# QKV weights in column blocks, made in their order of use while attention's first projections run

## The chip, the core and the metric

The kernel runs on one core of a Trainium2 chip. The core has five engines that work side by side, each through its own queue in order, and meet by semaphores: TensorE (PE in the profile; its weight loads are shown apart as PEld), VectorE (DVE), ScalarE (ACT), GpSimd (POOL) and SyncE (SP), which here issues the transfers. On-chip memory is SBUF (128 partitions); TensorE writes to PSUM. The metric is the device time of one execution in microseconds.

## The reference, cut to what matters

```python
# x: (8, 512, 1024) float32, H = 1024, 32 heads of 32
x = x + attention_a(layernorm(x), qkvw, qkvb, ow, ob)   # the stage of this change
x = x + ffn(layernorm(x), weight, bias, centroids, assignments)
x = x + attention_b(layernorm(x), bv_q, bv_k, bv_v)
x = x + ffn(layernorm(x), weight, bias, centroids, assignments)

def attention_a(x, qkvw, qkvb, ow, ob):
    q, k, v = split(x @ qkvw + qkvb)          # qkvw: (1024, 3072)
    probs = softmax(q @ k.T / sqrt(32))       # for each of 8 * 32 heads, 512 x 512
    return (probs @ v) @ ow + ob
```

## The kernel before

All products are made in float16 pairs. A float32 operand is scaled by a power of two and split into a high and a low half (hi = float16(s * w), lo = s * w - hi); a product of 128 x 512 by 1024 is then 24 matmuls (8 chunks of the contraction x 3 pairings of halves). The scale comes from the largest absolute value of the whole matrix: VectorE reduces each chunk (L255), GpSimd takes the maximum over partitions (partition_all_reduce, L231), VectorE makes the scale from it (scale_from_absmax, L71 to L75). The Q and K columns share one scale, the V columns have another.

**First phase** (L191 to L288). SyncE loads the weight in 8 row chunks for Q and K together (stg, 1 MB each, rows of 8 KB), then 8 for V (stgv, 512 KB each). VectorE reduces them; ScalarE writes the high halves (L285), VectorE the low ones (L245 for QK, L273 for V), GpSimd two of V's (L236, L238). They land in the arena, a buffer of 48 x 1024 float16 in each partition that all phases share: wqk in its parts 0 to 32, wv in 32 to 48. end_phase (L288) clears the semaphores and lets all engines meet.

**Second phase, attention** (from L291). SyncE asks for six tiles of x (128 x 1024 each, L501). For each: VectorE's bn_stats (L767) and bn_aggr, GpSimd's inv_deviation (L881, L883) and shift_x (L887), normalise_first on VectorE (L774), TensorE's transposes (turn_first, L622), ScalarE's hi_first (L689), VectorE's lo_first (L780, two operations a tile). Then TensorE runs the eight units of PRO: Q and K of head groups 0 and 1 (four units, L585), V of the first batch row, columns 0 to 512 (four units, L595). Each unit is 24 matmuls into the one bank proj_ps. ScalarE's leave (L681 for QK, L684 for V) copies it to stage, with the bias in bqk; GpSimd's split (L912, L914) makes the halves; SyncE stores and reloads those of Q and K for the heads. leave(u) of place i waits for the split of place i - 2; a unit waits until the bank is free (proj_free).

**Slots.** From there a hand-written schedule of one slot a head runs (SLOTS). Every slot has the score matmuls for the row maxima (max_scores, L536, banks ring_ps; VectorE L735), the scores (L546), the exponentials (ScalarE L666, L672; VectorE L753, GpSimd L859) and the weighted values (L563, L566); the projections of later groups (units_of) are laid between them, six matmuls at a time. Late in attention the output weight wo is loaded to the arena's parts 32 to 48, once the last V projection is done, and the feed-forward weight and small operands to parts 0 to 32, once the last Q and K projection is done.

GpSimd takes a partition_all_reduce also at L935 (late in attention) and L1396 and L1399 (in the stage behind it).

Of the kernel before, what the change touches and what calls it, by code (L numbers as in the profile page):

```python
# [127 lines left out]
def hybrid_layer(nc, x, qkvw, qkvb, ow, ob, bvq, bvk, bvv, fw, fb, cent, assign, out):  # L128
# [23 lines left out]
    with ExitStack() as top:  # L152
# [21 lines left out]
        def part16(a, z):  # L174
            return arena[:, a * H:z * H]
# [5 lines left out]
        wo = part16(32, 48).rearrange("p (a c n) -> p a c n", a=2, c=C)  # L181
        kq, signs, obias, cst, asg, asgf, ct0, fbx = (part32(2 * i, 2 * i + 2) for i in range(8))
        cst, asg, asgf, fbx = cst[0:NC], asg[0:NC].bitcast(I32), asgf[0:NC], fbx[0:33]
        fw_raw = part32(16, 32).rearrange("p (c n) -> p c n", c=C)


        with ExitStack() as p01:
            wqk = part16(0, 32).rearrange("p (a c n) -> p a c n", a=2, c=C)
            wv = part16(32, 48).rearrange("p (a c n) -> p a c n", a=2, c=C)
            bqk = sb(p01, "bqk", [P, 2 * H // P])  # L190
            exp_scale = sb(p01, "exp_scale", [P, 1])  # L191
            e_v = sb(p01, "e_v", [P, 1])
            s_v = sb(p01, "s_v", [P, 1])
# [4 lines left out]
            with ExitStack() as p0:  # L198
                stg = sb(p0, "stg", [P, C, 2 * H])
                stgv = sb(p0, "stgv", [P, C, H])  # L200
                mx = sb(p0, "mx", [P, 2, C + 1])
                bias = sb(p0, "bias", [P, 3 * H // P])
                m1 = sb(p0, "m1", [P, 2])
                m2 = sb(p0, "m2", [P, 2])
                es = sb(p0, "es", [P, 2])
                sc = sb(p0, "sc", [P, 2])
                qk_in, v_in, b_in = sem("qk_in"), sem("v_in"), sem("b_in")
                p0_max, p0_all, p0_sc, p0_hi, p0_id, p0_vs = (sem(n) for n in ("p0_max", "p0_all", "p0_sc", "p0_hi", "p0_id", "p0_vs"))
                V_LO_POOL = C // 4
                in_c = [sem(f"wc_in{c}") for c in range(C)]  # L210
                with nc.Block() as block:
                    @block.sync
                    def _(sp):
                        w_c = qkvw.rearrange("(c p) n -> c p n", p=P)
                        for c in range(C):
                            sp.dma_start(stg[:, c, :], w_c[c, :, 0:2 * H]).then_inc(in_c[c], 16)
                        for c in range(C):
                            sp.dma_start(stgv[:, c, :], w_c[c, :, 2 * H:3 * H]).then_inc(v_in, 16)

                    @block.gpsimd  # L220
                    def _(pool):
                        with nc.allow_non_contiguous_dma(reason="a small bias, one feature per partition"):
                            pool.dma_start(bias[:], qkvb.rearrange("(c p) -> p c", p=P)).then_inc(b_in, 16)
                        nc.gpsimd.memset(ident[:], 0.0).then_inc(p0_id, 1)
                        pool.wait_ge(p0_id, 1)
                        nc.gpsimd.affine_select(out=ident[:], in_=ident[:], compare_op=ALU.not_equal, fill=1.0,
                                                base=0, pattern=[[-1, P]], channel_multiplier=1).then_inc(p0_id, 1)

                        for i in range(2):
                            pool.wait_ge(p0_max, (C + 2) * (i + 1))  # L230
                            nc.gpsimd.partition_all_reduce(m2[:, i:i + 1], m1[:, i:i + 1], P, RMAX).then_inc(p0_all, 1)  # L231

                        pool.wait_ge(p0_sc, 6)
                        for c in range(V_LO_POOL):
                            pool.wait_ge(p0_hi, C + c + 1)
                            nc.gpsimd.tensor_scalar(stgv[:, c, :], stgv[:, c, :], sc[:, 1:2], None, ALU.mult).then_inc(p0_vs, 1)  # L236
                            pool.wait_ge(p0_vs, c + 1)
                            nc.gpsimd.tensor_tensor(wv[:, 1, c, :], stgv[:, c, :], wv[:, 0, c, :], ALU.subtract)  # L238

                    @block.vector  # L240
                    def _(dve):
                        def lo_qk(c):

                            dve.wait_ge(p0_hi, c + 1)
                            dve.scalar_tensor_tensor(out=wqk[:, 1, c, :], in0=stg[:, c, :], scalar=sc[:, 0:1],  # L245
                                                     in1=wqk[:, 0, c, :], op0=ALU.mult, op1=ALU.subtract)

                        for i, (w, b) in enumerate(((stg, bias[:, 0:2 * C]), (stgv, bias[:, 2 * C:3 * C]))):

                            for c in range(C):  # L250
                                if i == 0:
                                    dve.wait_ge(in_c[c], 16)
                                elif c == 0:
                                    dve.wait_ge(v_in, 16 * C)
                                dve.tensor_reduce(mx[:, i, c:c + 1], w[:, c, :], AX.X, ALU.max, apply_absolute_value=True).then_inc(p0_max, 1)  # L255
                            if i == 0:
                                dve.wait_ge(b_in, 16)
                            dve.tensor_reduce(mx[:, i, C:C + 1], b, AX.X, ALU.max, apply_absolute_value=True).then_inc(p0_max, 1)
                            dve.wait_ge(p0_max, (C + 2) * i + C + 1)
                            dve.tensor_reduce(m1[:, i:i + 1], mx[:, i, :], AX.X, ALU.max).then_inc(p0_max, 1)  # L260
                            dve.wait_ge(p0_all, i + 1)
                            scale_from_absmax(dve, m2[:, i:i + 1], es[:, i:i + 1], sc[:, i:i + 1], p0_sc, 3 * i)
                            if i == 0:

                                for c in range(C // 2):
                                    lo_qk(c)
                        dve.tensor_scalar(bqk[:], bias[:, 0:2 * C], sc[:, 0:1], None, ALU.mult)
                        for c in range(C // 2, C):
                            lo_qk(c)

                        for c in range(V_LO_POOL, C):
                            dve.wait_ge(p0_hi, C + c + 1)
                            dve.scalar_tensor_tensor(out=wv[:, 1, c, :], in0=stgv[:, c, :], scalar=sc[:, 1:2],  # L273
                                                     in1=wv[:, 0, c, :], op0=ALU.mult, op1=ALU.subtract)
                        dve.tensor_copy(e_v[:], es[:, 1:2])
                        dve.tensor_copy(s_v[:], sc[:, 1:2])
                        dve.scalar_tensor_tensor(out=exp_scale[:], in0=es[:, 0:1], scalar=float(HD) ** -0.5,
                                                 in1=es[:, 0:1], op0=ALU.mult, op1=ALU.mult)

                    @block.scalar  # L280
                    def _(act):
                        for i, (w, wd) in enumerate(((stg, wqk), (stgv, wv))):
                            act.wait_ge(p0_sc, 3 * (i + 1))
                            for c in range(C):
                                nc.scalar.activation(wd[:, 0, c, :], w[:, c, :], ACT.Copy, scale=sc[:, i:i + 1]).then_inc(p0_hi, 1)  # L285

            end_phase()


            with ExitStack() as p1:  # L290
                xt = sb(p1, "xt", [P, 2, H])  # L291
# [121 lines left out]
                def x_first(t):  # L413
                    two = (e32[:], ehi[:].rearrange("p a t s -> p a (t s)").bitcast(F32).rearrange("p a (h s) -> p a h s", h=2),
                           elo[:].rearrange("p a t s -> p a (t s)").bitcast(F32).rearrange("p a (h s) -> p a h s", h=2))[t // 2]
                    return two[:, t % 2].rearrange("p h s -> p (h s)")
# [7 lines left out]
                with nc.Block() as block:  # L424

                    @block.sync
                    def _(sp):
                        def load_x(n):
                            if n >= FIRST + 2:
                                sp.wait_ge(proj_full, place["T", n - 2, 1] + 1)  # L430
                            sp.dma_start(xt[:, n % 2], x_t[n // T, n % T]).then_inc(xt_in, 16)
# [31 lines left out]
                        def out_weight(s):  # L463
# [17 lines left out]
                            if 0 <= c < C:  # L481
                                sp.wait_ge(proj_full, place["V", B - 1, T - 1, 1] + 1)
                                sp.wait_ge(wo_out, 16 * C)
                                sp.dma_start(wo[:, :, c], wo_d[c]).then_inc(wo_in, 16)
# [15 lines left out]
                        for t in range(FIRST):  # L500
                            sp.dma_start(x_first(t), x_t[t // T, t % T]).then_inc(x0_in[t], 16)  # L501
# [1580 lines left out]
```

## Time and profile before

| | |
|---|---|
| median of 3 runs | 3384.23 us (3383.88 to 3388.84) |
| the profiled execution | 3387.1 us, span 3385.3 us |
| granted TensorE clock over the span | 0.99 |
| TensorE busy | 3205.6 us, 95% |
| VectorE, ScalarE, GpSimd busy | 65%, 52%, 57% |
| first phase | 0 to 73.7 us |
| last stage, chain that ended last | TensorE |

The profile lists each engine's instructions with start and duration in us from the span's start. A group names line, engine, operation, written tile and read tiles. "Idle before" is the time in which the engine stood still ahead of an instruction, with what released it. The granted clock (PEclk) is in shares of TensorE's full speed.

### The profile page before, as it was taken

How to read it: one execution, taken by the hardware profiler on the slowest of the kernel's cores; microseconds unless marked ns; L12 is line 12 of the kernel's file. 1: busy time of each engine (PE TensorE's matmuls, PEld its weight loads, DVE VectorE, ACT ScalarE, POOL GpSimd, SP SyncE). 2: the span in 40 equal slices, each digit the busy share in tenths (PEclk: the TensorE clock that was granted, in tenths of full speed). 3: DMA queues.
4: the chain of work that ended last, by engine and by line, in shares of the span. 5: the costliest groups of instructions: out<-in, count | busy, mean ns of one | idle time of the engine just before them, and what ended most of it. 6: DMA issues, size and time to landing. Idle time of an engine off the chain costs nothing. (4 is left out here: it accounts for less than half of the span.)

```text
span 3385.3 us, 62616 instructions
## 1 busy us (share of the span) xinstructions
PE 3205.6 (95%) x24256; PEld 1711.9 (51%) x24256; DVE 2189.8 (65%) x3858; ACT 1745.6 (52%) x2125; POOL 1927.5 (57%) x2065
## 2 busy tenths in 40 slices
PE   0899999999999999999999899998999999999999
PEld 0455555555555555555444455554555555554443
DVE  8377777777777777777788587774455555542311
ACT  3277777777777777777677422221345555552000
POOL 2277777777777777777676422221565555540422
PEclk9999999999999999999999899999999999999999
DMA  4122222222222222222334644443223222223533
GB/s 186 41 60 70 67 70 68 78 64 70 72 64 70 64 73 64 76 70 69 108 111 140 192 166 158 156 157 112 75 88 104 102 100 100 88 76 144 204 137 137
DMA packets 277524, 342.95 MB, mean 101 GB/s; under 512 B 92236, under 2 KB 206924, under 8 KB 276206
## 3 DMA queue, kind: packets, MB, share of 16 engines
q1 hardware_dynamic: 272558, 322.16, 30.0%
q10 hardware_dynamic: 4608, 16.78, 1.3%
q8 instruction: 194, 3.18, 0.4%
q14 instruction: 100, 0.82, 0.1%
q0 software_dynamic: 64, 0.01, 0.0%
HBM read 199.91 MB, written 138.42 MB: 100 GB/s over the span
## 5 line engine op out<-in xcount | busy, mean ns | idle before, releaser
L735 DVE TENSOR_REDUCE nmax<-ring_ps 128x1 f32<-128x512 f32 x1024 | 676.2, 685 | 418.2 <-PE ring_ps L536 415.6
L859 POOL TENSOR_TENSOR elo<-e,ehi 128x1024 f16<-128x1024 f32 x256 | 669.6, 2616 | 355.7 <-ACT ehi L672 355.7
L666 ACT ACTIVATE e<-st_ps,exp_scale 128x1024 f32<-128x1024 f32 x512 | 570.7, 1115 | 373.2 <-PE st_ps L546 308.2
L585 PE MATMUL proj_ps<-xnT,arena 128*128 128x512 f16 x3072 | 750.5, 381 | 3.3 <-DVE xnT L780 2.5
L672 ACT ACTIVATE ehi<-st_ps,exp_scale 128x1024 f16<-128x1024 f32 x512 | 568.6, 1110 | 0.0
L1596 PE MATMUL f_ps<-wT,fxT 128*128 128x512 f16 x1920 | 435.6, 381 | 2.9 <-DMA fxT<-xT_scratch 2.9
L585 PEld LDWEIGHTS proj_ps<-xnT,arena 128*128 128x128 f16 x3072 | 272.3, 97 | 286.9 <-ACT stage L684 11.7
L536 PE MATMUL ring_ps<-ks,qs 96*128 96x512 f16 x1024 | 397.2, 388 | 17.0 <-DVE nmax L735 17.0
L546 PE MATMUL st_ps<-qs,ks 98*128 98x512 f16 x1024 | 392.6, 383 | 12.0 <-ACT ehi L672 11.3
L563 PEld LDWEIGHTS ctx_ps<-v_sb,ehi 128*128 128x128 f16 x4096 | 312.5, 97 | 155.1 <-DVE sums L762 39.3
L563 PE MATMUL ctx_ps<-v_sb,ehi 128*128 128x65 f16 x4096 | 372.0, 192 | 14.0 <-DVE sums L762 12.7
L595 PE MATMUL proj_ps<-arena,xnT 128*128 128x512 f16 x1536 | 370.8, 378 | 2.9 <-ACT stage L684 2.1
L566 PE MATMUL ctx_ps<-v_sb,elo 128*128 128x33 f16 x4096 | 355.8, 179 | 0.0
L1086 PE MATMUL o_ps<-arena,cT 128*128 128x512 f16 x1536 | 344.0, 381 | 3.2 <-DVE cT L1315 3.2
L753 DVE TENSOR_TENSOR elo<-e,ehi 128x1024 f16<-128x1024 f32 x256 | 333.3, 1302 | 1.1 <-ACT ehi L672 1.1
L566 PEld LDWEIGHTS ctx_ps<-v_sb,elo 128*128 128x128 f16 x4096 | 274.7, 97 | 116.1 <-issue 3.1
L1596 PEld LDWEIGHTS f_ps<-wT,fxT 128*128 128x128 f16 x1920 | 187.4, 98 | 208.8 <-issue 6.0
L1086 PEld LDWEIGHTS o_ps<-arena,cT 128*128 128x128 f16 x1536 | 149.8, 98 | 172.9 <-DVE cT L1315 4.0
L2019 POOL TENSOR_TENSOR arena<-arena,fm 128x512 f32<-128x512 f32 x64 | 83.6, 1306 | 229.3 <-DVE fm L1872 229.3
L595 PEld LDWEIGHTS proj_ps<-arena,xnT 128*128 128x128 f16 x1536 | 135.4, 97 | 144.0 <-ACT stage L684 3.5
L1386 POOL TENSOR_SCALAR rstd<-mv 128x1 f32<-128x1 f32 x32 | 7.1, 223 | 301.1 <-DVE mv L1264 286.6
L536 PEld LDWEIGHTS ring_ps<-ks,qs 96*128 96x128 f16 x1024 | 115.8, 113 | 97.4 <-DVE nmax L735 34.5
(240 smaller groups left out, 4616.3 us busy)
## 6 DMA issues: line engine op xcount, KB each, us to landing
qk_scratch<-qk_hl SPq DMA_DIRECT2D x128, 256.0 KB, 2.3
fxT<-xT_scratch SPq DMA_DIRECT2D x64, 512.0 KB, 3.5
qs<-qk_scratch SPq DMA_DIRECT2D x192, 128.0 KB, 2.6
ks<-qk_scratch SPq DMA_DIRECT2D x192, 128.0 KB, 2.9
arena<-x_scratch SPq DMA_DIRECT2D x48, 512.0 KB, 4.3
ctx_scratch<-ctx SPq DMA_DIRECT2D x64, 256.0 KB, 3.0
xb<-in_L_attn_a_x_dram SPq DMA_DIRECT2D x32, 512.0 KB, 4.4
x_scratch<-xb SPq DMA_DIRECT2D x32, 512.0 KB, 2.6
```

What stands on the lines that cost most here:

```text
L536: pe.matmul(ring_ps[:, ring_max(h, c) % 2, :], qs_v[0:3 * HD, h % RING, c, :], ks[0:3 * HD, h % RING, :], start=True, stop=True).then_inc( ...
L546: mm = pe.matmul(st_ps[:, c // 2, c % 2, :], ks[0:3 * HD + 2, h % RING, P * c:P * c + P], qs[0:3 * HD + 2, h % RING, :], start=True, stop= ...
L563: pe.matmul(ctx_v[:, t, :], ehi[:, h % 2, c, P * t:P * t + P], v_sb[:, c, hh, :], start=(c == 0 and t == 0), stop=False, skip_group_check= ...
L566: mm = pe.matmul(ctx_v[:, t, 0:HD + 1], elo[:, h % 2, c, P * t:P * t + P], v_sb[:, c, hh, 0:HD + 1], start=False, stop=(c == T - 1), skip_ ...
L585: mm = pe.matmul(proj_ps[:], wqk[:, wp, c, H * qk + P * g:H * qk + P * g + P], xnT[:, b % 2, xp, c, :], start=(n == 0), stop=(n == 23))
L595: mm = pe.matmul(proj_ps[:], xnT[:, b % 2, xp, c, P * t:P * t + P], wv[:, wp, c, S * half:S * half + S], start=(n == 0), stop=(n == 23))
L666: nc.scalar.activation(e32[:, half], st_ps[:, half], ACT.Exp, scale=exp_scale[:, 0:1]).then_inc(e32_done, 1)
L672: nc.scalar.activation(ehi[:, h % 2, 2 * half:2 * half + 2, :], st_ps[:, half], ACT.Exp, scale=exp_scale[:, 0:1]).then_inc(ehi_done, 1)
L735: dve.tensor_reduce(nmax[:, h % 2, c:c + 1], ring_ps[:, ring_max(h, c) % 2, :], AX.X, ALU.max, negate=True).then_inc(ring_free, 1)
L859: nc.gpsimd.tensor_tensor(elo[:, h % 2, 2:4, :], e32[:, 1], ehi[:, h % 2, 2:4, :], ALU.subtract).then_inc(elo_pool, 1)
L1086: mm = pe.matmul(o_ps[:, half, :], cT[:, n % 2, xp, c, :], wo[:, wp, c, 512 * half:512 * half + 512], start=(i == 0), stop=(i == 23))
L1596: pe.matmul(f_ps[:, half, :], fxT[:, t % 2, xp, c, :], wT[:, wp, c, cols], start=(n == 0), stop=False)
```

## The change

The first phase goes; its work is done inside attention's block. The weight is cut into six column blocks, BLOCKS = QK 0, V 0, QK 1, V 1, QK 2, QK 3. A QK block holds 256 columns of Q and 256 of K (two head groups), a V block 512 columns. Block j has its halves in the arena's parts 8j to 8j + 8, and its raw float32 data, loaded ahead, in the place of block j + 1 (the last one in e32 and ehi). It is worked in two halves of 128 x 2048: weight_hi(j) on ScalarE, weight_lo(j) on VectorE; the high half of block j + 1 overwrites raw data of block j and waits for its low half.

SyncE asks for x tiles 0 to 3 first, then for the eight QK pieces, then the four V pieces (1 MB each; 1 KB runs for QK, 2 KB for V), then for x tiles 4 and 5. The layer norm's normalise_first goes from VectorE to ScalarE. The V scale is made once block QK 0 is finished. Units wait for their own block only (qkv_lo). Two banks take turns in PRO (proj_ps and ring_ps 1), so that a unit waits for the leave of the one before the last; the slots wait until all eight are left. The memset of ks goes to GpSimd. The output weight (wo_part) now lies in the places of the V blocks and the feed-forward weight in parts 32 to 48, under the same waits as before.

```diff
-        wo = part16(32, 48).rearrange("p (a c n) -> p a c n", a=2, c=C)
-        fw_raw = part32(16, 32).rearrange("p (c n) -> p c n", c=C)
+        def wo_part(c):
+            return part16(8 + 16 * (c // 4), 16 + 16 * (c // 4)).rearrange("p (a c n) -> p a c n", a=2, c=4)[:, :, c % 4]
+        fw_raw = part32(32, 48).rearrange("p (c n) -> p c n", c=C)
...
+            BLOCKS = (("QK", 0), ("V", 0), ("QK", 1), ("V", 1), ("QK", 2), ("QK", 3))
+            def half_of(j, i, a):
+                return part16(8 * j + 4 * i + 2 * a, 8 * j + 4 * i + 2 * a + 2)
...
-            end_phase()
...
+                def bank(u):
+                    return ring_ps[:, 1] if place[u] < len(PRO) and place[u] % 2 else proj_ps[:]
...
-                        for t in range(FIRST):
+                        for t in range(T):
                             sp.dma_start(x_first(t), x_t[t // T, t % T]).then_inc(x0_in[t], 16)
+                        for n, (j, i) in enumerate(LOADS):
+                            piece = raw_of(j, i).rearrange("p (c n) -> p c n", c=C if BLOCKS[j][0] == "QK" else C // 2)
+                            sp.dma_start(piece, raw_from(j, i)).then_inc(qkv_in[n], 16)
+                        for t in range(T, FIRST):
+                            sp.wait_ge(x0_turned, 2 * (t - T) + 2)
+                            sp.dma_start(x_first(t), x_t[t // T, t % T]).then_inc(x0_in[t], 16)
...
                         for i, u in enumerate(PRO):
                             unit(u, 0, 24)
-                            if i < 2:
-                                turn_first(T + i)
-                        pe.wait_ge(const_done, 4)
+                            if i in (3, 4):
+                                turn_first(T + i - 3)
+                        pe.wait_ge(const_done, 3)
+                        pe.wait_ge(ks_ones, 1)
                         pe.wait_ge(x0_lo, 2 * FIRST)
+                        pe.wait_ge(qkv_lo, 2 * NB)
+                        pe.wait_ge(proj_free, len(PRO))
...
+                        def weight_hi(j):
+                            v = BLOCKS[j][0] == "V"
+                            act.wait_ge(p0_sc, 6 if v else 3)
+                            for i in range(2):
+                                wait(act, qkv_lo, 2 * (j - 1) + i + 1)
+                                nc.scalar.activation(half_of(j, i, 0), raw_of(j, i), ACT.Copy, scale=sc[:, v:v + 1]).then_inc(qkv_hi, 1)
...
+                        weight_hi(0)
+                        act.wait_ge(bqk_done, 1)
+                        leave(PRO[0])
+                        weight_hi(1)
+                        leave(PRO[1])
+                        normalise_first(4)
+                        normalise_first(5)
+                        weight_hi(2)
+                        leave(PRO[2])
+                        leave(PRO[3])
+                        hi_first(4)
+                        weight_hi(3)
+                        leave(PRO[4])
+                        hi_first(5)
+                        weight_hi(4)
+                        leave(PRO[5])
+                        weight_hi(5)
+                        leave(PRO[6])
+                        leave(PRO[7])
...
+                        for t in range(T):
+                            stats_first(t)
+                        for n in range(C):
+                            weight_max(n)
+                            if n < T:
+                                lo_first(n)
+                        weight_scale(0)
...
+                        weight_lo(0)
+                        for n in range(C, C + 4):
+                            weight_max(n)
+                        weight_scale(1)
+                        weight_lo(1)
+                        stats_first(4)
+                        stats_first(5)
+                        weight_lo(2)
+                        lo_first(4)
+                        weight_lo(3)
+                        lo_first(5)
+                        weight_lo(4)
+                        weight_lo(5)
...
+                        def weight_all(kind):
+                            pool.wait_ge(p0_max, C + 8 if kind else C + 2)
+                            nc.gpsimd.partition_all_reduce(m2[:, kind:kind + 1], m1[:, kind:kind + 1], P, RMAX).then_inc(p0_all, 1)
...
+                        nc.gpsimd.memset(ks[3 * HD:3 * HD + 2], ONES_ROW).then_inc(ks_ones, 1)
+                        pool.wait_ge(ks_ones, 1)
+                        weight_all(0)
+                        split(PRO[0])
+                        weight_all(1)
+                        split(PRO[1])
+                        for t in range(T, FIRST):
+                            inv_deviation(t)
+                            shift_x(t)
+                        for u in PRO[2:]:
                             split(u)
```

## Rows read from the trace of the kernel before

**Rows 1.** The page: span, busy tenths in 40 slices, one of its groups.

```profile
span 3385.3 us, 62616 instructions
...
PE   0899999999999999999999899998999999999999
...
L585 PEld LDWEIGHTS proj_ps<-xnT,arena 128*128 128x128 f16 x3072 | 272.3, 97 | 286.9 <-ACT stage L684 11.7
```

**Rows 2.** Windows: stretch and length, busy us by engine, clock, DMA share, GB/s.

```profile
200.00:1600.00 1400.00, 1387.12 (x12134) 737.31 (x12131) 1061.99 (x1928) 1014.08 (x1054) 1084.32 (x1103) 1.00 0.24 69
```

**Rows 3.** Timeline, 0 to 75 us: start, us, engine, line, operation [idle before].

```profile
13.18 2.29 DVE L255 TENSOR_REDUCE mx<-stg 128x1 f32<-128x2048 f32 x1 [0.64 <-DMA stg<-_L_attn_a_attn_qkvw_dram]
...
25.64 2.29 DVE L255 TENSOR_REDUCE mx<-stg 128x1 f32<-128x2048 f32 x1 [0.22 <-DMA stg<-_L_attn_a_attn_qkvw_dram]
...
29.31 15.25 ACT L285 ACTIVATE arena<-stg,sc 128x2048 f16<-128x2048 f32 x8 [27.23 <-DVE sc L75]
31.42 9.14 DVE L245 SCALAR_TENSOR_TENSOR arena<-stg,sc,arena 128x2048 f16<-128x2048 f32 x4 [2.14 <-ACT arena L285]
...
49.94 0.35 POOL L231 PARTITION_ALL_REDUCE m<-m  x1 [21.23 <-DVE m L260]
...
50.88 8.43 ACT L285 ACTIVATE arena<-stgv,sc 128x1024 f16<-128x1024 f32 x8 [6.32 <-DVE sc L75]
...
73.69 0.80 SPq L501 DMA_DIRECT2D e<-in_L_attn_a_x_dram  x2
```

**Rows 4.** Timeline, 75 to 147 us.

```profile
78.27 1.29 DVE L767 BATCH_NORM_STATS2 st<-e 128x6 f32<-128x512 f32 x2
...
81.00 0.27 POOL L887 TENSOR_SCALAR shift<-mv,rstd 128x1 f32<-128x1 f32 x1
...
84.34 1.28 DVE L780 TENSOR_TENSOR xnT<-st_ps,xnT 128x512 f16<-128x512 f32 x2
...
95.61 7.85 PE L585 MATMUL proj_ps<-xnT,arena 128*128 128x512 f16 x24 [2.54 <-DVE xnT L780]
...
104.24 5.35 PE L585 MATMUL proj_ps<-xnT,arena 128*128 128x512 f16 x24
104.25 0.61 POOL L912 CAST qk_hl<-stage 128x512 f16<-128x512 f32 x1 [8.82 <-ACT stage L681]
...
104.95 1.16 POOL L914 TENSOR_TENSOR qk_hl<-stage,qk_hl 128x512 f16<-128x512 f32 x1
...
109.43 1.04 PE L622 MATMUL st_ps<-ident,elo 128*128 128x128 f32 x8
...
145.97 0.60 PE L536 MATMUL ring_ps<-ks,qs 96*128 96x512 f16 x2
```

**Rows 5.** Line 694, the norm of later x tiles on ScalarE: ns min/median/max.

```profile
L694 ACT ACTIVATE xt<-xt,shift,rstd x26: 1235/1238/1254, 191.9 to 1554.0; 128x1024 f32<-128x1024 f32 x26
```

**Rows 6.** Timeline of GpSimd around its all-reduces.

```profile
57.50 5.31 POOL L236 TENSOR_SCALAR stgv<-stgv,sc 128x1024 f32<-128x1024 f32 x1 [7.22 <-ACT arena L285]
...
1675.31 0.38 POOL L935 PARTITION_ALL_REDUCE m2o<-m1o  x1 [5.88 <-issue]
...
1683.21 1.14 POOL L914 TENSOR_TENSOR qk_hl<-stage,qk_hl 128x512 f16<-128x512 f32 x1 [6.98 <-issue]
...
2050.06 0.38 POOL L1399 PARTITION_ALL_REDUCE m<-m  x1 [8.14 <-issue]
```

**Rows 7.** Windows of TensorE alone: stretch, length, busy, clock, DMA share, GB/s.

```profile
152.00:154.00 2.00, 2.00 (x5) 0.50 0.08 1
...
1684.00:1688.00 4.00, 0.00 (x0) 0.56 0.39 111
```

**Rows 8.** Windows of all engines in the old load and behind attention.

```profile
13.20:33.20 20.00, 0.00 (x0) 0.00 (x0) 16.17 (x12) 3.89 (x3) 0.38 (x1) 1.00 1.01 417
...
1960.00:2060.00 100.00, 100.00 (x692) 56.14 (x691) 78.29 (x137) 21.33 (x48) 24.05 (x25) 1.00 0.49 164
```

**Rows 9.** Line 273, VectorE beside GpSimd: ns min/median/max.

```profile
L273 DVE SCALAR_TENSOR_TENSOR arena<-stgv,sc,arena x6: 1273/2095/3137, 60.1 to 69.6; 128x1024 f16<-128x1024 f32 x6
```

More of the change, by code:

```diff
@@ L190, in hybrid_layer, with wv @@
+            def wv(half, a, c):
+                return half_of(BLOCKS.index(("V", half)), c // 4, a)[:, S * (c % 4):S * (c % 4) + S]
             bqk = sb(p01, "bqk", [P, 2 * H // P])
             exp_scale = sb(p01, "exp_scale", [P, 1])
-            e_v = sb(p01, "e_v", [P, 1])
-            s_v = sb(p01, "s_v", [P, 1])
             e_o = sb(p01, "e_o", [P, 1])
             bv_hl = sb(p01, "bv_hl", [P, 2, C], F16)
[L198 to L285, printed above, removed]
@@ L573, in unit @@
                             if a == 0:
-                                wait(pe, proj_free, place[u])
+                                wait(pe, proj_free, place[u] - 1 if place[u] < len(PRO) else place[u])
                             if u[0] == "QK":
@@ L588, in unit @@
                                 b, t, half = u[1:]
+                                if a == 0 and b == 0:
+                                    pe.wait_ge(qkv_lo, 2 * BLOCKS.index(("V", half)) + 2)
                                 if a == 0 and half == 0 and T * b + t < FIRST:
@@ L594, in unit @@
                                     c, (xp, wp) = n // 3, ((0, 0), (0, 1), (1, 0))[n % 3]
-                                    mm = pe.matmul(proj_ps[:], xnT[:, b % 2, xp, c, P * t:P * t + P],
-                                                   wv[:, wp, c, S * half:S * half + S], start=(n == 0), stop=(n == 23))
+                                    mm = pe.matmul(bank(u), xnT[:, b % 2, xp, c, P * t:P * t + P],
+                                                   wv(half, wp, c), start=(n == 0), stop=(n == 23))
                             if z == 24:
@@ L633, in turn @@
                             mm.then_inc(proj_full, 1)
+                        pe.wait_ge(p0_id, 2)
                         for t in range(T):
@@ new lines, in weight_scale @@
+                        def weight_scale(kind):
+                            k, done = (C, C + 2) if kind == 0 else (4, C + 8)
+                            if kind == 0:
+                                dve.wait_ge(b_in, 16)
+                            dve.tensor_reduce(mx[:, kind, k:k + 1], bias[:, 2 * C * kind:2 * C * kind + (C if kind else 2 * C)], AX.X, ALU.max,
+                                              apply_absolute_value=True).then_inc(p0_max, 1)
+                            dve.wait_ge(p0_max, done - 1)
+                            dve.tensor_reduce(m1[:, kind:kind + 1], mx[:, kind, 0:k + 1], AX.X, ALU.max).then_inc(p0_max, 1)
+                            dve.wait_ge(p0_all, kind + 1)
+                            scale_from_absmax(dve, m2[:, kind:kind + 1], es[:, kind:kind + 1], sc[:, kind:kind + 1], p0_sc, 3 * kind)
@@ new lines, in weight_lo @@
+                        def weight_lo(j):
+                            v = int(BLOCKS[j][0] == "V")
+                            for i in range(2):
+                                dve.wait_ge(qkv_hi, 2 * j + i + 1)
+                                dve.scalar_tensor_tensor(out=half_of(j, i, 1), in0=raw_of(j, i), scalar=sc[:, v:v + 1],
+                                                         in1=half_of(j, i, 0), op0=ALU.mult, op1=ALU.subtract).then_inc(qkv_lo, 1)
+                        for t in range(T):
+                            stats_first(t)
@@ L914, in split @@
                             nc.gpsimd.tensor_tensor(lo, src, hi, ALU.subtract).then_inc(split_done, 1)
+                        def weight_all(kind):
+                            pool.wait_ge(p0_max, C + 8 if kind else C + 2)
+                            nc.gpsimd.partition_all_reduce(m2[:, kind:kind + 1], m1[:, kind:kind + 1], P, RMAX).then_inc(p0_all, 1)
+                        with nc.allow_non_contiguous_dma(reason="a small bias, one feature per partition"):
+                            pool.dma_start(bias[:], qkvb.rearrange("(c p) -> p c", p=P)).then_inc(b_in, 16)
+                        nc.gpsimd.memset(ident[:], 0.0).then_inc(p0_id, 1)
+                        pool.wait_ge(p0_id, 1)
+                        nc.gpsimd.affine_select(out=ident[:], in_=ident[:], compare_op=ALU.not_equal, fill=1.0,
+                                                base=0, pattern=[[-1, P]], channel_multiplier=1).then_inc(p0_id, 1)
                         pool.wait_ge(const_done, 1)
-                        for t in range(FIRST):
+                        for t in range(T):
                             inv_deviation(t)
                             shift_x(t)
-                        for u in PRO:
+                        pool.wait_ge(shift_done, T)
+                        nc.gpsimd.memset(ks[3 * HD:3 * HD + 2], ONES_ROW).then_inc(ks_ones, 1)
[8 more added lines that the diff above has]
+                        for u in PRO[2:]:
                             split(u)
```

95 lines of the change are left out of this document (61 added, 34 removed).

## The prediction

> **What bounds the kernel now.** The page first: TensorE is busy for eight or nine tenths of every slice but the first [rows 1]; in the long middle of attention it works for 1387 of 1400 us [rows 2]. So a time saved elsewhere counts only where TensorE has nothing to do, and that is the first slice. The timeline of the first 150 us shows it. Until 73.7 us the first phase brings the whole QKV weight, finds its largest values and splits it; only then is x asked for [rows 3], and the first projection runs at 95.61. Eight projections in a row follow, and the first score matmul, from which on TensorE sets the pace, starts at 145.97 [rows 4]. I forecast that mark for the changed kernel; what follows it is the same work in the same order, bound by TensorE, so I let the end move by as much.
>
> **Load and largest value.** x (2 MB) now goes first, then the QK pieces of 1 MB. Before, the third megabyte was in use at 13.18 [rows 3], so the first QK piece is there at 13.2 (the arrivals before it are an estimate: 4.4 to 10.2 for x, from the 4.6 us that x0 took from its request at 73.69 to its statistics at 78.27 [rows 3, 4] and 1.25 to 1.5 us for each half megabyte). VectorE now also does lo_first (two operations, 1.28 us [rows 4]) behind each of the first four reductions. The reductions take 2.29 us [rows 3], so the eighth starts at 13.2 + 7 x 2.29 + 4 x 1.28 = 34.3. The layer norm of x fits ahead of that (3.0 us from statistics to shift [rows 4]), except that the third and fourth turn wait for lo_first(0) and (1); nobody waits for them before 44. What it costs if the load is slower: the last QK piece must be there at 34.3, which leaves 3.0 us for each megabyte. Packets shrink from 8 KB to 1 KB. In the old load the queues moved 417 GB/s at full share (2.5 us a megabyte); the stage behind attention, with many small packets, 164 GB/s at a share of 0.49, so 335 (3.1 us) [rows 8]; attention 69 at 0.24, so 288 (3.6 us) [rows 2]. I take at most 3.0, nearest the middle row, so no cost; the bounds are 0 and 5.3 us. From the start of the last reduction to ScalarE's first split before: 25.64 to 29.31, 3.67 us [rows 3]. So ScalarE starts on block 0 at 38.0, VectorE 2.11 us later [rows 3], and two lo operations of 2.3 us end at 44.7. The constants moved to GpSimd (ks memset) lie in its idle time between 13 and 34.
>
> **First projection at 44.7 instead of 95.6.** It started on a slow clock before: 24 matmuls in 7.85 us against 5.35 for the next [rows 4]. TensorE now idles for over 20 us ahead of it, so I take 7.85 again (bounds 5.35 and 10.4, all 24 at twice the 0.216 us of the fast ones, 104.24 to 109.43 [rows 4]): end 52.6. ScalarE's leave lies between that and GpSimd's split (103.46 to 104.25 before), which takes 1.86 us (to 106.11 [rows 4]): 55.2.
>
> **The wait that the change adds.** GpSimd's queue is now weight_all(0), split(PRO[0]), weight_all(1), split(PRO[1]), the norm of x tiles 4 and 5. The trace shows that GpSimd stands still whenever it goes from ordinary work to PARTITION_ALL_REDUCE or back. Toward it: 5.9 us (ahead of 1675.31) with the DMA queues quiet, 8.1 at 2050.06 with them busy. Back: 7.2 at 57.50 although ScalarE's piece, the named releaser, was ready at 52.0 (50.88 + 1.1 [rows 3]), and 7.0 at 1683.21 [rows 6]. The old kernel ran its two all-reduces back to back and paid one such stop, in the shadow of VectorE. The new one puts a split between them. The V reductions (4 x 2.29 behind 44.7) and the small ones are done at 54.3, but the all-reduce waits for the split until 55.2 and then for the stop of 5.9: 61.1 (bounds 0, were the stop hidden, and 8.1; I take 5.9 because the weight load is over by then). Behind it are queued: ScalarE's weight_hi(1), thus leave(PRO[1]), thus projection 3; VectorE's lo(1), then the statistics of x tiles 4 and 5. The stops around all-reduce 0 are hidden: toward it between 20 and 34, back between 38 and 53.3.
>
> By the Trainium skill's page "GPSIMD Engine Reference", section 2.1 (Instruction dispatch), the first call of a freshly loaded GpSimd routine pays about 6 us with nothing to see in the profile. Read strictly, the second all-reduce is no first call and would pay nothing (rival 1); but the third and the fifth of this trace, at 1675 and 2050, pay in full [rows 6], so I side with the rows.
>
> **From there to the mark.** ScalarE starts block 1 at 61.1 + 0.94 = 62.0 (49.94 to 50.88 before [rows 3]). VectorE's second lo ends at 62.0 + 2.1 + 4.6 = 68.7. Statistics of tile 4 from 68.7 and of tile 5 from 70.2, shift 3.0 us on (78.27 to 81.27 [rows 4]): 73.2. GpSimd's stop back ends at 61.5 + 7.0 = 68.5 and its split at 70.4, just in time. The norm now runs on ScalarE at 1.24 us [rows 5], and sits ahead of weight_hi(2) and leave(PRO[2]) in its queue: norm 5 ends at 74.4, two splits of 1.95 at 78.3, leave(PRO[2]) at 79.0. Projection 2 ended long before (about 63), yet projection 4 must wait for that bank: it starts at 79.0. Projection 3 and the turn of tile 4 (1.04 us) end by 74.5, so TensorE has 4.5 idle us. Before, the short score matmuls from 145.97 on, each waiting for VectorE, were followed by a granted clock of 0.50 (152 to 154), and an idle stretch at 1684 to 1688 by 0.56, partly at the lower level [rows 7]; that level is 1.2 GHz, full is 2.4. I take the slow 7.85 for projection 4 (bounds 5.35 and 10.4): 86.9. Turn 5: 87.9. Projections 5 to 7 use alternate banks, so the leave between two projections (0.8 us) is gone: 3 x 5.2 (104.24 to 109.43 [rows 4]) = 15.6, end 103.5. Leave of the last, 0.2 + 0.6, which now must end before the first score matmul because it shares a bank with it: mark at 104.5. VectorE's lo chain and ScalarE's weight_hi(3) to (5) fit in beside: the last lo is due about 100.7. Their slack is some 3 us; GpSimd's splits can eat of it, since lo operations that took 1.27 us alone took up to 3.14 beside GpSimd [rows 9].
>
> **Sum:** 145.97 - 104.5 = 41.5 us less. Nothing else is priced: the barrier of 1 us is inside it, and the new places of the output and feed-forward weights in the arena keep their waits. The profiled execution took 3387.1 us, 2.9 above the median of 3384.2; I forecast the median: 3384.2 - 41.5 = 3342.7.
>
> **Rivals.**
> 1. The stop does not land on the path (no stop, or hidden behind another chain): 5.9 less, and the clock may stay up at projection 4, 2.5 less: 3334 to 3340. For it: at 49.94 an all-reduce paid nothing, but right behind another one [rows 3]. Against: each all-reduce that follows ordinary work pays [rows 6]. 10%.
> 2. The 1 KB load is the bound: at 3.1 to 3.6 us a megabyte the scale is late by 1 to 5.3 us: 3344 to 3348; with the 8.1 stop 3350. For it: the two rows with small packets. Against: those rows mix reads and writes, and the pieces here only read. 20%. By the Trainium skill's page "DMA: Bandwidth & Descriptors", Specifications, packets from 512 B up go at line rate, which would rule this rival out; no row here shows 1 KB reads alone.
> 3. The other side, slower: the projections read their weights from blocks with another stride, those of Q and K are 3072 matmuls, nearly all inside attention [rows 1]. LDWEIGHTS takes 97 ns and hides under a matmul of 216. If each grew by over 15.7 ns ((41.5 + 6.8) / 3072), the kernel would be over 0.2% slower; at 20 ns 3384.2 - 41.5 + 61.4 = 3404. Against: width, type and contiguity of what one LDWEIGHTS reads stay. 2%.
> 4. The change does not do what it says: the chains of block 1 to 5 on VectorE and ScalarE hold the projections so long that the mark hardly moves, or attention hands the gain back to something tied to the clock: 3384. It would take 40 us of delay beyond the worked chain, which counts all of the 24 large operations. 2%.
> The forecast, with its own bounds of the clock and the stop (3339 to 3346), has the remaining 66%.
>
> **Range.** From 3336 (into rival 1, and the old load shows a lull from 7 to 9 us that may fall elsewhere, 2 us) to 3350 (rival 2): 80%. A measurement of this kernel can tell about 0.2%, 6.8 us, from no change. Faster by more than that: 66 + 10 + 20% = 96%; same 2%; slower 2%.
>
> **What would show it.** First projection at 45 (load and VectorE chain); an all-reduce at 61, a gap of about 6 us in front of it and of 7 behind it; ScalarE's leave of projection 2 at 79 with its bank full since 63; slow first matmuls in projection 4; first score matmul at 104.5, and attention from there unchanged in length. Wrong if the QK reductions wait for DMA at 3 us or more apart, if the all-reduce follows the split at once, or if attention's length differs.

## The result and the profile after

The changed kernel runs in 3363.44 us (median of 4 runs, 3362.31 to 3364.41) against 3385.25 for the kernel before in the same comparison: the ratio is 0.9934, 95% interval 0.992 to 0.9947. It is faster, by about half of what I had forecast (3342.7, range 3336 to 3350). In the profiled executions the span went from 3385.3 to 3361.3 us, 24.0 less; the first score matmul, the mark that I had forecast at 104.5, went from 145.97 [rows 4] to 119.63, 26.3 less, and 2.3 us were lost behind it.

The page of the changed kernel, to be held against [rows 1]: the first slice (0 to 84 us) now has three tenths of TensorE. In the second slice the granted clock is below full; windows give 0.88 from 84 to 168 us, against 0.98 for the second slice of the kernel before.

```profile
span 3361.3 us, 62605 instructions
...
PE   3899999999999999999899899998999999999999
...
PEclk9899999999999999999998899998999999999999
```

Its timeline from 35 to 120 us (start, us, engine, line, operation, idle before), beside [rows 3] and [rows 4]:

```profile
35.09 2.29 DVE L813 TENSOR_REDUCE mx<-ehi 128x1 f32<-128x2048 f32 x1 [0.70 <-DMA ehi<-_L_attn_a_attn_qkvw_dram]
...
38.86 3.89 ACT L672 ACTIVATE arena<-arena,sc 128x2048 f16<-128x2048 f32 x2 [15.84 <-DVE sc L75]
...
45.57 6.91 PE L538 MATMUL proj_ps<-xnT,arena 128*128 128x512 f16 x24 [23.18 <-DVE arena L830]
...
53.34 0.61 POOL L941 CAST qk_hl<-stage 128x512 f16<-128x512 f32 x1 [15.07 <-ACT stage L640]
...
61.55 1.15 POOL L943 TENSOR_TENSOR qk_hl<-stage,qk_hl 128x512 f16<-128x512 f32 x1 [7.60 <-issue]
...
68.77 0.38 POOL L947 PARTITION_ALL_REDUCE m<-m  x1 [6.08 <-issue]
...
69.75 3.89 ACT L672 ACTIVATE arena<-arena,sc 128x2048 f16<-128x2048 f32 x2 [16.47 <-DVE sc L75]
...
84.56 1.14 POOL L943 TENSOR_TENSOR qk_hl<-stage,qk_hl 128x512 f16<-128x512 f32 x1 [7.62 <-issue]
...
87.14 2.55 ACT L664 ACTIVATE elo<-elo,shift,rstd 128x1024 f32<-128x1024 f32 x2 [12.93 <-POOL shift L916]
...
94.10 8.23 PE L550 MATMUL proj_ps<-arena,xnT 128*128 128x512 f16 x24 [3.70 <-ACT stage L640]
...
119.63 0.60 PE L487 MATMUL ring_ps<-ks,qs 96*128 96x512 f16 x2 [0.88 <-ACT stage L643]
```

Up to the first projection (45.57) the forecast holds within a microsecond. Then look at GpSimd. A split is two operations, a CAST and a TENSOR_TENSOR that belong together. In split 0 there are 7.60 us between them, then 6.08 us ahead of the all-reduce, and in split 1 again 7.62 us between the two. ScalarE stands still for 16.47 us for the second scale and for 12.93 us for the shift of x tile 4. The view of line 943 has one more kind of row:

```profile
L943 POOLq MODIFY_POOL_CONFIG  x6: 7/11/76, 54.0 to 1653.7; - x6
```

After the first 5 us, every such instruction in all the traces stands between an all-reduce and ordinary operations, one pair for each change in either direction (e3, which has no all-reduce in this stage, has none before 1623.9 us), so I read it as the order to GpSimd to change its kind of work. The first of line 943 stands at 54.0, behind the CAST of split 0, not behind the all-reduce at 37.9. So the stop on the way back does not begin when the all-reduce ends. It begins in front of the first operation that needs it, and the CAST is none.

### The profile page after: what moved, and what is told of

The parts are those of the page before. It is cut to its first block and busy times, and to the rows that moved or that the text cites. A ratio compares the mean times of both kernels' runs of the same rounds, so it can differ in the third digit from the quotient of the medians.

```text
span 3361.3 us, 62605 instructions
## 1 busy us (share of the span) xinstructions
PE 3213.0 (96%) x24256; PEld 1715.8 (51%) x24256; DVE 2181.3 (65%) x3843; ACT 1751.7 (52%) x2127; POOL 1927.7 (57%) x2062
## 5 line engine op out<-in xcount | busy, mean ns | idle before, releaser
L538 PE MATMUL proj_ps<-xnT,arena 128*128 128x512 f16 x3024 | 738.5, 380 | 23.2 <-DVE arena L830 23.2
L943 POOL TENSOR_TENSOR qk_hl<-stage,qk_hl 128x512 f16<-128x512 f32 x128 | 150.8, 1178 | 32.7 <-issue 22.7
```

The costliest lines, as they stand in the source:

```text
L538: mm = pe.matmul(bank(u), wqk(g, qk, wp, c), xnT[:, b % 2, xp, c, :], start=(n == 0), stop=(n == 23))
```

## The experiments

My theory after this reading: three stops of GpSimd, 7.6 + 6.1 + 7.6 us, lie on the path, of which the forecast had one. Rivals: the low clock, VectorE and ScalarE in each other's way, the load with its short runs. The changed kernel was not timed again beside the experiments. Each was timed with the kernel before, whose median was 3386.75 us there (e1 to e4) and 3386.24 us (e5 to e7), against 3385.25 in the result. So a difference between an experiment and the changed kernel is uncertain by one or two microseconds, and the timelines carry the finer readings.

**e1_early_back.** One small ordinary operation behind each all-reduce, so that the way back starts at once.

```diff
                             nc.gpsimd.partition_all_reduce(m2[:, kind:kind + 1], m1[:, kind:kind + 1], P, RMAX).then_inc(p0_all, 1)
+                            nc.gpsimd.tensor_tensor(tiny[:, kind:kind + 1], mhalf[:], mhalf[:], ALU.add)
```

> The changed kernel with one small ordinary GpSimd operation right behind each all-reduce, so that GpSimd's stop on the way back to ordinary work runs while nobody waits, as my forecast had taken it. Theory (both stops of GpSimd sit on the path, 7.6 us inside split 0 and again inside split 1): the second all-reduce starts at 61.3 instead of 68.8, split 1 loses its stop of 7.6 us, leave of projection 2 ends near 80 instead of 94, first score matmul near 105.5 instead of 119.6, time 14 us less, 3349. Rival (the 15 us beyond my forecast come from the low clock and from VectorE and ScalarE getting in each other's way): within 1 us of 3363.

Measured: 3350.08 us (3347.74 to 3352.19), ratio to the kernel before 0.9891 (0.9877 to 0.9906), 13.4 us less than the changed kernel. Its timeline:

```profile
45.98 0.18 POOL L949 TENSOR_TENSOR tiny<-mhalf 128x1 f32<-128x1 f32 x1 [7.70 <-issue]
...
61.09 0.38 POOL L948 PARTITION_ALL_REDUCE m<-m  x1 [5.81 <-issue]
...
68.48 0.36 POOL L949 TENSOR_TENSOR tiny<-mhalf 128x1 f32<-128x1 f32 x1 [7.01 <-issue]
...
79.04 7.34 PE L551 MATMUL proj_ps<-arena,xnT 128*128 128x512 f16 x24 [4.57 <-ACT stage L641]
...
103.67 0.60 PE L488 MATMUL ring_ps<-ks,qs 96*128 96x512 f16 x2 [0.88 <-ACT stage L644]
```

All stops are still there and about as long (7.70, 5.81 and 7.01 us), only elsewhere: the two on the way back now run while nobody waits for GpSimd. The all-reduce starts at 61.09 (forecast 61.1), projection 4 at 79.04 (forecast 79.0), the mark is at 103.67 (forecast 104.5). This one added operation makes the way to the mark the one that I had forecast. The time is not: 3350.08 us is 13.4 less, as the theory said (14), but still 7.4 above my forecast of 3342.7; that part is taken up below. The theory of the stops stands; the rivals would have left the time where it was.

**e2_swap.** The two all-reduces back to back.

```diff
                         weight_all(0)
+                        weight_all(1)
                         split(PRO[0])
-                        weight_all(1)
                         split(PRO[1])
```

> The changed kernel with the two all-reduces back to back in GpSimd's queue (weight_all(1) ahead of split(PRO[0])). Theory (stops): the second all-reduce starts at 54.6 instead of 68.8, no stop in front of it; one stop of 7.6 us is left, inside split 0, in the shadow of block 1; first score matmul near 100, time 19 to 20 us less, 3344. Rival (it was the split in front of the all-reduce as such, or the low clock): at most 2 us less.

Measured: 3343.35 us (3342.71 to 3345.55), ratio 0.9874 (0.9857 to 0.989), 20.1 us less than the changed kernel. Timeline:

```profile
54.94 0.35 POOL L947 PARTITION_ALL_REDUCE m<-m  x1 [16.38 <-DVE m L822]
55.16 0.67 POOL L941 CAST qk_hl<-stage 128x512 f16<-128x512 f32 x1
...
62.76 1.15 POOL L943 TENSOR_TENSOR qk_hl<-stage,qk_hl 128x512 f16<-128x512 f32 x1 [6.92 <-issue]
...
99.48 0.60 PE L487 MATMUL ring_ps<-ks,qs 96*128 96x512 f16 x2 [0.88 <-ACT stage L643]
```

Two lines in another order give almost as much again as the whole change. The second all-reduce follows the first with no stop (it waits for VectorE alone), and the CAST runs right behind it; the stop comes only in front of the TENSOR_TENSOR, 6.92 us, under block 1.

**e3_tensor_max.** No all-reduce at all in this stage; TensorE and VectorE find the largest value.

```diff
+                            dve.tensor_copy(ctx[:, kind, 0], m1[:, kind:kind + 1].to_broadcast([P, P])).then_inc(wide_done, 1)
+                            dve.wait_ge(max_turned, kind + 1)
+                            dve.tensor_reduce(m2[:, kind:kind + 1], ctx_ps[:, P * kind:P * kind + P], AX.X, ALU.max).then_inc(p0_all, 1)
...
+                            pe.transpose(ctx_ps[:, P * kind:P * kind + P], ctx[:, kind, 0], ident[:]).then_inc(max_turned, 1)
...
-                        weight_all(0)
                         split(PRO[0])
-                        weight_all(1)
                         split(PRO[1])
```

> The changed kernel without any all-reduce in this stage: VectorE spreads the 128 maxima over a row, TensorE turns it (the second one in the middle of projection 1), VectorE reduces. No change of GpSimd's kind of work is left before the slots. Theory (stops): second scale near 56 instead of 69.7, no gap of over 2 us inside a split, first score matmul near 99, time 20 to 21 us less, 3342.5. If the stop belonged to the split operations themselves (their first use) and not to the all-reduce, split 0 would still show 7 us, and the time would be near that of the swapped queue.

Measured: 3337.57 us (3336.66 to 3339.28), ratio 0.9855 (0.9841 to 0.987). The splits show no stop:

```profile
53.88 0.61 POOL L954 CAST qk_hl<-stage 128x512 f16<-128x512 f32 x1 [36.29 <-ACT stage L649]
54.58 1.16 POOL L956 TENSOR_TENSOR qk_hl<-stage,qk_hl 128x512 f16<-128x512 f32 x1
...
57.13 3.89 ACT L681 ACTIVATE arena<-arena,sc 128x2048 f16<-128x2048 f32 x2 [3.39 <-DVE sc L75]
...
99.46 0.59 PE L488 MATMUL ring_ps<-ks,qs 96*128 96x512 f16 x2 [0.88 <-ACT stage L652]
```

So the stop belongs to the change of work and not to the split. The mark (99.46) is that of the swapped queue, since there the one stop left was hidden; but the time is 25.9 us below the changed kernel's where I had expected 20 to 21, and 5.8 below that of e2 where I had expected 1 to 2. That is taken up below.

**e4_tensor_max_order.** As e3, with another order in ScalarE's queue.

```diff
                         leave(PRO[1])
+                        leave(PRO[2])
                         normalise_first(4)
                         normalise_first(5)
+                        leave(PRO[3])
                         weight_hi(2)
-                        leave(PRO[2])
-                        leave(PRO[3])
                         hi_first(4)
```

> As the one before, and in ScalarE's queue the leave of projection 2 stands ahead of the norms of x tiles 4 and 5 and the leave of projection 3 ahead of block 2's split. Theory (what comes late next is ScalarE's order: projection 4 waits for a bank that has been full for 10 us): TensorE runs projections 0 to 7 with no gap over 2 us, the clock stays up, first score matmul near 92, time 27 us less than the changed kernel, 3336. Rival (VectorE's chain of low halves is next in line): its last low half ends later than projection 7, the mark is 96 or later, and TensorE waits for VectorE at the end.

Measured: 3335.82 us (3332.72 to 3336.53), ratio 0.9848 (0.9833 to 0.9862). The time is as expected, the way there only in part. It is 1.8 us below that of e3, little more than the spread of the runs.

```profile
70.88 5.34 PE L551 MATMUL proj_ps<-arena,xnT 128*128 128x512 f16 x24
...
95.91 0.60 PE L488 MATMUL ring_ps<-ks,qs 96*128 96x512 f16 x2 [3.27 <-DVE arena L843]
```

Projection 4 starts at 70.88, 3.0 us earlier than in e3, on the fast clock (5.34 us). But the mark comes at 95.91 and not at 92: TensorE waits 3.27 us for VectorE's last low half, as the rival said (it put the mark at 96 or later). With GpSimd's stops gone and ScalarE's order mended, VectorE is next in line.

**e5_long_runs.** The eight QK pieces are read as whole rows of 8 KB, which puts other columns in each block.

```diff
+                            if n < C:
+                                sp.dma_start(raw_of(j, i), qkvw[P * n:P * n + P, 0:2 * H]).then_inc(qkv_in[n], 16)
+                                continue
```

> The changed kernel with the eight QK pieces read as whole rows of 8 KB (128 weight rows by 2048 columns) into the same places, so that its projections use the wrong columns; all work is the same. Theory (1 KB runs cost bandwidth, but the load is hidden): the load moves 417 GB/s instead of 349 while it lasts, the wait of 0.7 us before the last QK reduction goes, the first scale comes 0.7 us earlier, everything behind it moves by that, time within 1.5 us of 3363. Rival (the load bounds this stage): the first scale comes 3 us or more earlier.

Measured (one run): 3361.1 us, 2.3 less than the changed kernel, and further from 3363 than the 1.5 us that I had allowed; VectorE's last QK reduction starts at 33.75 with no wait, the all-reduce at 36.53 and not at 37.88, 1.35 us earlier, twice the 0.7 that I had expected. 0.70 of it is the wait for the last piece; the first reduction also starts 0.43 us sooner (13.61 against 14.04). Windows of VectorE in the load, changed kernel first, then e5 (stretch, length, busy, clock, DMA share, GB/s):

```profile
14.00:33.90 19.90, 19.82 (x15) 1.00 1.10 349
```

```profile
14.00:33.90 19.90, 19.90 (x16) 0.54 1.02 413
```

The 1 KB runs do cost bandwidth, 349 against 413 GB/s, 3.0 against 2.5 us a megabyte. That is just what the reductions allow: the load and VectorE are nearly level there, and a bound of 3 us or more did not show. The time itself says little: in this run the two stops on the way back took 6.68 and 6.86 us against 7.60 and 7.62, and that is 1.7 us without any part of the load.

**e7_one_bank.** All eight projections in one PSUM bank again.

```diff
-                    return ring_ps[:, 1] if place[u] < len(PRO) and place[u] % 2 else proj_ps[:]
+                    return proj_ps[:]
...
-                                wait(pe, proj_free, place[u] - 1 if place[u] < len(PRO) else place[u])
+                                wait(pe, proj_free, place[u])
```

> The changed kernel with all eight projections in one PSUM bank, as in the kernel before. Theory: with ScalarE's leaves queued behind block splits, each projection waits for the leave of the one before; projection 2 starts at 74 instead of 57, projection 3 at 94 instead of 74, and the last four are 0.8 us further apart: first score matmul near 130 instead of 119.6, time 10 us more, 3373. Rival (the two stops hide it): only the four gaps of 0.8, 3 us more.

Measured: 3372.12 us (3369.44 to 3372.28), ratio 0.9956 (0.9941 to 0.9971): 8.7 us more than the changed kernel (expected 10), the mark at 127.30 instead of 119.63 (expected near 130). Projection 2 started at 74.91 and projection 3 at 94.24, as worked out. The second bank carries about a third of the change's gain (0.9956 against 0.9934 of the kernel before), because ScalarE's leaves now queue behind weight splits.

**e6_warm_start.** As e4, with idle matmuls at the start of the slots.

```diff
+                        def idle_work(n):
+                            for _ in range(n):
+                                pe.matmul(ctx_ps[:], xnT[:, 0, 0, 0, 0:P], xnT[:, 0, 0, 0, :], start=True, stop=True)
+
+                        idle_work(14)
                         pe.wait_ge(qkv_lo, 2 * NB)
...
                                 max_scores(s + 2, c)
+                                if s < 0:
+                                    idle_work(2)
```

> The kernel of e4_tensor_max_order with idle matmuls into a free bank: 14 while TensorE waits for VectorE's last low half, and two behind each of the eight first score matmuls. Theory (what the stage behind the mark lost against the kernel before is the granted clock, low from 97 to 107 us there): no stretch at half clock around the first slots, time 3 to 5 us less than 3335.8. Rival (the clock falls for another reason, or the slots wait for row transfers anyway): same time within 1 us, or more by the idle matmuls' 1 us.

Measured: 3330.88 us (3330.66 to 3333.25), ratio 0.9839 (0.9825 to 0.9852), 4.9 us less than e4 in the medians and 3.7 in the profiled spans (3334.8 and 3331.1). Windows of TensorE from 90 to 112 us, e4 first, then e6:

```profile
90.00:112.00 22.00, 17.39 (x57) 0.77 0.01 0
```

```profile
90.00:112.00 22.00, 21.66 (x99) 1.00 0.09 24
```

Thirty useless matmuls kept the clock at 2.4 GHz and paid for themselves. Not all of the difference is theirs. The last projection started 0.6 us sooner already (86.69 against 87.29), after a projection 0 of 7.08 us in place of 8.31. From there to the mark 0.3 us are gained, and from the mark to the third exponential 2.35 (14.65 against 17.00 us). So 2.7 us are traced to the idle matmuls; the ranges of the two kernels' runs touch (e4 from 3332.72, e6 up to 3333.25). This is the fastest of all: 1.6% below the kernel before, 1.0% below the changed one.

## Why the prediction was wrong

**The step that failed** is in "The wait that the change adds": "The stops around all-reduce 0 are hidden: toward it between 20 and 34, back between 38 and 53.3", and in the next part "GpSimd's stop back ends at 61.5 + 7.0 = 68.5 and its split at 70.4". I had the stop back begin when the all-reduce ends. It begins in front of the first operation that needs it, which is the TENSOR_TENSOR inside the split. So both ways back lie on the path, where the forecast had put them at nothing. The chain shows what followed, beside the forecast and beside e1, which puts the way back where I had it:

| us | forecast | changed kernel | e1 |
|---|---|---|---|
| first ScalarE split of block 0 | 38.0 | 38.86 | 38.87 |
| projection 0 starts | 44.7 | 45.57 | 45.58 |
| second all-reduce | 61.1 | 68.77 | 61.09 |
| ScalarE on block 1 | 62.0 | 69.75 | 62.07 |
| split 1 ends | 70.4 | 85.70 | 70.64 |
| projection 4 starts | 79.0 | 94.10 | 79.04 |
| first score matmul | 104.5 | 119.63 | 103.67 |

So 7.7 us came from split 0 and 7.6 more from split 1, 15.1 at the mark. The evidence was in the trace of before and I misread it: [rows 6] has the TENSOR_TENSOR of a split at 1683.21 with a stop of 6.98 us in front, and what stood between it and the all-reduce at 1675.31 was that split's own CAST:

```profile
1675.57 0.67 POOL L912 CAST qk_hl<-stage 128x512 f16<-128x512 f32 x1
```

I took the row as "the next operation behind an all-reduce"; it was the second. At 57.50 the next operation was itself one that needs the change of work, so there the stop could start at once, and I made that one the rule.

**The rest of the miss.** A second step failed, "so I let the end move by as much". Behind the mark the changed kernel needs 3241.7 us against 3239.4, so it cost 2.3 us. 2.2 us more lie between the difference of the spans (24.0) and that of the medians (21.8), and 1.1 in the median of before, which came out at 3385.25 where I had started from 3384.2. e1 shows what this is worth: with the stops where the forecast had them, its mark came 0.8 us before the forecast, but it needs 3244.2 us behind it, 4.9 more than the kernel before, and with 3.3 us between spans and medians it ends at 3350.08, at the upper end of my range. So even with the stops right, the number would have been 7.4 us too low.

**What held.** The load and VectorE's chain up to the first projection, within 0.9 us, of which 0.7 is the wait for the last QK piece: 1 KB pieces came 3.0 us apart, the most that I had allowed. Projection 0 on a slow clock: 6.91 us instead of the 7.85 taken. (In the experiments it took from 6.78 to 8.31 us, so how far the low clock reaches into it is chance.) The stop toward the all-reduce: 6.08 for 5.9. That projection 4 waits for the leave of projection 2 behind norms and a split in ScalarE's queue, and starts on the slow clock: 8.23 us for 7.85. VectorE's lo chain had the slack that I gave it (its last low half ends at 116.43, 3.2 us before the mark). In e1 the mark came at 103.67, so the sum of the other terms up to the mark was right to 0.8 us.

**The rivals.** Rival 1 (no stop on the path) was wrong in the other direction: there were three. By the Trainium skill, "GPSIMD Engine Reference", section 2.1 (Instruction dispatch), the first call to a freshly loaded kernel pays about 6 us more. I had said that this, read strictly, lets the second all-reduce pay nothing. Here the second all-reduce behind ordinary work paid 6.08 us, and in e2 the second one right behind the first paid nothing. It is the alternation that costs, and the way back as well. Rival 2 wanted 3.1 us a megabyte or more; 3.0 came, the most that the forecast itself allowed, and the first scale was late by 0.7 us for it. The rule of the Trainium skill's page "DMA: Bandwidth & Descriptors", Specifications, that packets from 512 B up go at line rate does not hold here (349 against 413 GB/s). Rival 3: a LDWEIGHTS of the Q and K projections takes 97 ns in both kernels and their matmul 380 ns against 381 in the mean, so the new places of the weights cost nothing. (TensorE's busy time rose by 7.4 us in all; the low clock ahead of and behind the mark lengthens matmuls.) Rival 4, "It would take 40 us of delay beyond the worked chain": 15 came. A smaller form of it should have had a chance of its own, since the delays of this chain over three engines added up: of the 15.3 us at the end of split 1, 15.1 arrived at the mark. The range reached 7.3 us above the forecast; one unpriced way back of 7.6 us would already have used it up.

**Behind the mark.** Counted from the mark, ScalarE's exponentials of the slots show where the time goes. The third comes 0.8 us later than in the kernel before, the 25th 4.6 us later, and at the end of the span 2.3 of them are left; where the rest is given back is not traced.

The first place is the start of the slots, on the low clock. In the changed kernel the granted clock over 114 to 136 us was 0.84, in the kernel before over 140 to 162 it was 0.92:

```profile
114.00:136.00 22.00, 19.02 (x68) 0.84 0.02 0
```

The second place lies 77 us behind the mark, and costs 3.7 us. One slot there has VectorE's subtraction of exponentials beside GpSimd's. In e2 it reads:

```profile
176.77 2.13 POOL L888 TENSOR_TENSOR elo<-e,ehi 128x1024 f16<-128x1024 f32 x1 [0.62 <-ACT ehi L631]
177.01 2.97 DVE L746 TENSOR_TENSOR elo<-e,ehi 128x1024 f16<-128x1024 f32 x1
...
180.64 0.41 PE L487 MATMUL ring_ps<-ks,qs 96*128 96x512 f16 x1 [1.96 <-DVE nmax L728]
...
183.16 0.63 PE L487 MATMUL ring_ps<-ks,qs 96*128 96x512 f16 x1
```

In e3 the same two operations overlap as well, but in the other order:

```profile
176.78 1.21 DVE L755 TENSOR_TENSOR elo<-e,ehi 128x1024 f16<-128x1024 f32 x1
176.85 3.12 POOL L901 TENSOR_TENSOR elo<-e,ehi 128x1024 f16<-128x1024 f32 x1 [0.62 <-ACT ehi L640]
```

The engine that starts first keeps its time (1.21 us for VectorE, 2.13 for GpSimd), and the other pays (2.97 or 3.12). GpSimd has room to pay and VectorE has not: with VectorE late, TensorE waits 1.96 us, and from 182 to 184 us its granted clock is 0.51, so that a score matmul takes 0.63 us instead of 0.38. The kernel before, e3, e4 and e6 have VectorE first in this slot; the changed kernel and e1 have GpSimd first, as e2 does, and all three pay. In e2 VectorE comes late because its copy of sums, the operation before, starts after 0.20 us of standing still, for which the trace names no releaser; that cause stays open. From the mark to the late all-reduce e2 needs 1533.1 us and e3 1530.0, so 3.1 us of e3's unexpected gain lie in this stretch.

## What to carry to other kernels

When a change puts an operation of another kind into an engine's queue, look for the stop on both sides of it, and for the exact operation in front of which each stop stands; price every alternation, not each kind once. Keep rare GpSimd routines such as the all-reduce together, or place a small ordinary operation behind each so that the way back runs while nobody waits. Where VectorE and GpSimd subtract at nearly the same time, look at which of them starts first: a few tenths of a microsecond decided who paid 1 to 2 us here. And when a chain crosses three engines, give the range room for at least one more delay of the largest kind found.

## What the runs showed of the hardware

- GpSimd stops for 5.8 to 6.1 us on the way to an all-reduce and for 6.9 to 7.7 us on the way back (the early rows of the changed kernel, e1 and e2; in e5 one way back took 6.68). A CAST runs directly behind an all-reduce without a stop (55.16 in e2); a TENSOR_TENSOR does not.
- TensorE's clock rewards useless work: with 14 idle matmuls in a wait and two behind each of the eight first score matmuls, the granted clock over 90 to 112 us was 1.00 instead of 0.77. 2.7 us of the saving are traced to them, although nothing of them is used.
- VectorE and GpSimd hold each other up, and the first to start keeps its time. Over attention in e2 the two subtractions overlap 211 times. VectorE is first in 205, with a median of 1.22 us, and GpSimd's then is 2.91; GpSimd is first in six, with 2.13, and VectorE's median is 2.98. The same holds where VectorE makes low halves: a CAST of 0.61 us that started behind one took 2.5 to 2.7 us and a TENSOR_TENSOR of 1.15 up to 3.2 us, while the TENSOR_TENSOR at 81.72 in e1, begun 0.73 us before VectorE's operation, kept its 1.16 us. Beside VectorE's reductions (a CAST at 53.34 in the changed kernel) GpSimd kept its 0.61 us. In e1, from the projections' splits:

```profile
79.11 2.52 POOL L942 CAST qk_hl<-stage 128x512 f16<-128x512 f32 x1 [5.77 <-ACT stage L641]
...
85.57 3.08 POOL L944 TENSOR_TENSOR qk_hl<-stage,qk_hl 128x512 f16<-128x512 f32 x1
```
